# Windowed attention's softmax in the first stage: the exponentials taken by group of 64 keys on ScalarE, in place of a shift and a sum on VectorE

## What is computed

```python
attn = jnp.einsum('bhnd,bhmd->bhnm', q, k)
bias = bias_table[REL_IDX.reshape(-1)].reshape(N, N, NH).transpose(2, 0, 1)
attn = jax.nn.softmax(attn + bias[None], axis=-1)
out = jnp.einsum('bhnm,bhmd->bhnd', attn, v)
```

## Time and profile before

| | us |
|---|---|
| median of three runs | 798.73 |
| lowest and highest | 797.12, 801.46 |
| the profiled execution | 798.17 |
| its span (first to last instruction) | 796.4 |
| granted clock of TensorE, mean of the span | 0.906 |

### The profile page before, as it was taken

The page is one execution under the profiler, slowest core; times in us unless marked ns, Lnnn a source line. Parts: engine busy times, 40 slices in busy tenths (PEclk is TensorE's granted clock), DMA queues, the critical chain, the costliest instruction groups (busy, mean ns, idle before and its releaser), DMA issues.

```text
span 796.4 us, 20147 instructions
## 1 busy us (share of the span) xinstructions
PE 639.5 (80%) x8800; PEld 538.0 (68%) x8800; DVE 498.0 (63%) x1102; ACT 328.0 (41%) x510; POOL 208.4 (26%) x193
## 2 busy tenths in 40 slices
PE   5355797979797979687479576899999899989776
PEld 5345576868686868665368465678787787868665
DVE  2267678687878787821445353558677776847455
ACT  3134343443435343400697514453536355342420
POOL 0100000000000000000468542635446373633330
PEclk8575899999999999898599798889999999989898
DMA  5120301010101000000112403213140413220000
GB/s 206 54 74 1 119 14 38 15 38 16 37 16 37 2 2 2 2 1 12 55 32 63 66 14 54 51 18 64 18 81 15 68 34 48 49 33 2 14 15 14
DMA packets 28263, 29.76 MB, mean 37 GB/s; under 512 B 1936, under 2 KB 22544, under 8 KB 28048
## 3 DMA queue, kind: packets, MB, share of 16 engines
q1 hardware_dynamic: 28176, 28.49, 15.8%
HBM read 22.19 MB, written 6.29 MB: 36 GB/s over the span
## 4 chain that ended last, share of the span: by engine, by line
PE 31%; DVE 7%; ACT 5%; POOL 3%; DMA 3%; issue 2%; SPq 1%; DVEq 0%; POOLq 0%; ACTq 0%
PE ps L214 17%; PE ps L1050 3%; PE ps L1002 3%; DMA ks<-rope_scratch 2%; PE ps L1028 2%; DVE mx L1318 2%; PE ps L1031 2%; POOL hl L1224 1%; PE ps L1034 1%; PE ps L1005 1%; PE ps L913 1%; ACT wide L1138 1%; DVE acc L1408 1%; SPq L897 1%; DVE st L1260 1%
## 5 line engine op out<-in xcount | busy, mean ns | idle before, releaser
L1238 POOL TENSOR_TENSOR e2l<-prob,e2h 128x1536 f16<-128x1536 f32 x32 | 98.7, 3103 | 18.5 <-ACT e2h L1173 18.5
L214 PE MATMUL ps<-secondh,ch_moe 128*128 128x256 f16 (+1 forms) x320 | 82.6, 266 | 3.3 <-DVE cl_moe L1271 3.0
L214 PE MATMUL ps<-yh,wconvh 128*128 128x256 f16 x288 | 80.7, 280 | 3.3 <-DVE yl L755 3.3
L214 PE MATMUL ps<-secondh,cl_moe 128*128 128x256 f16 (+1 forms) x320 | 82.7, 265 | 0.0
L1318 DVE TENSOR_REDUCE mx<-ps 128x2 f32<-128x512 f32 (+1 forms) x96 | 65.4, 682 | 27.1 <-PE ps L1005 27.1
L214 PE MATMUL ps<-secondl,ch_moe 128*128 128x256 f16 (+1 forms) x320 | 82.4, 264 | 0.0
L214 PE MATMUL ps<-yh,wconvl 128*128 128x256 f16 x288 | 80.9, 281 | 0.0
L214 PE MATMUL ps<-yl,wconvh 128*128 128x256 f16 x288 | 80.5, 280 | 0.0
L635 POOL TENSOR_TENSOR rstd<-mv,eps 128x4 f32<-128x4 f32 x8 | 1.6, 201 | 265.7 <-DVE mv L660 265.7
L1167 ACT ACTIVATE prob<-ps 128x1536 f32<-128x1536 f32 x32 | 46.5, 1452 | 54.3 <-PE ps L1034 54.3
L1408 DVE SCALAR_TENSOR_TENSOR acc<-ps,gate,acc 128x256 f32<-128x256 f32 x112 | 49.0, 479 | 21.7 <-PE ps L214 21.7
(11 more groups left out here) (217 smaller groups left out, 2117.5 us busy)
## 6 DMA issues: line engine op xcount, KB each, us to landing
weights_stage<-in_second SPq DMA_DIRECT2D x6, 684.0 KB, 4.2
qs<-rope_scratch SPq DMA_DIRECT2D x48, 64.0 KB
ks<-rope_scratch SPq DMA_DIRECT2D x48, 64.0 KB
weights_stage<-in_wconv SPq DMA_DIRECT2D x6, 384.0 KB, 3.7
xw<-in_xw SPq DMA_DIRECT2D x8, 256.0 KB, 2.7
xc<-in_xc SPq DMA_DIRECT2D x8, 256.0 KB, 2.6
rope_scratch<-rh SPq DMA_DIRECT2D x8, 256.0 KB, 2.3
rope_scratch<-rl SPq DMA_DIRECT2D x8, 256.0 KB, 2.3
```

The source lines that it names most:

```text
L214: last = nc.tensor.matmul(out_ap, lhs[x], rhs[w], start=done == 0, stop=done == n - 1)
L1238: nc.gpsimd.tensor_tensor(el[n % 2][:], prob[n % 2][:], eh[n % 2][:], ALU.subtract).then_inc(e2_lo, 1)
```

## The change

In `scores`, VectorE no longer subtracts the maxima from the tile: it changes the sign of the 16 maxima of each half (an instruction over 128 x 16 in place). ScalarE then takes the exponential of each group of 64 keys by an instruction of its own, with the negated maximum of that group as the bias (a pointer to a column of 128 numbers), and each of these instructions also writes the sum of its 64 results to a column of `sums`. There are 16 for each half, 32 for each image and 256 in all, where there were 2 and 16. The semaphore `exp_done` is raised by the last of each sixteen. In `turn`, VectorE's sum and the wait on it go.

```diff
+                rows = prob[:].rearrange("p (g m) -> p g m", m=WTOK)
                 for at in range(2):
-                    act.wait_ge(shifted[p], i * 2 + at + 1)
-                    e = prob[:, at * 2 * BANK:(at + 1) * 2 * BANK]
-                    nc.scalar.activation(e, e, ACT.Exp).then_inc(exp_done[p], 1)
+                    act.wait_ge(negated[p], i * 2 + at + 1)
+                    for g in range(at * 16, at * 16 + 16):
+                        last = nc.scalar.activation(rows[:, g], rows[:, g], ACT.Exp, bias=mx[:, g:g + 1],
+                                                    accum_out=sums[:, g:g + 1])
+                    last.then_inc(exp_done[p], 1)
...
                 for at in range(2):
                     dve.wait_ge(max_done[p], i * 2 + at + 1)
-                    nc.vector.tensor_tensor(rows[:, at], rows[:, at],
-                                            mx[:, at * 16:(at + 1) * 16].unsqueeze(2).to_broadcast([P, 16, WTOK]),
-                                            ALU.subtract).then_inc(shifted[p], 1)
+                    columns = mx[:, at * 16:(at + 1) * 16]
+                    nc.vector.tensor_scalar(columns, columns, -1.0, None, ALU.mult).then_inc(negated[p], 1)
...
-                rows = prob[:].rearrange("p (g m) -> p g m", m=WTOK)
                 dve.wait_ge(exp_done[p], i * 2 + 2)
-                nc.vector.tensor_reduce(sums[:], rows, op=ALU.add, axis=AX).then_inc(sum_done[p], 1)
-                dve.wait_ge(sum_done[p], i + 1)
                 nc.vector.reciprocal(rs[:], sums[:]).then_inc(recip_done[p], 1)
```

More of the change, by code:

```diff
@@ L360, in windows @@
         (x_loaded, dct_done, stats_done, mv_done, eps_added, rstd_done, norm_done, tr_done, affine_done, xh_done,
-         xl_done, qk_done, qkh_done, qkl_done, v_done, vh_done, vl_done, scores_done, biased, max_done, shifted,
+         xl_done, qk_done, qkh_done, qkl_done, v_done, vh_done, vl_done, scores_done, biased, max_done, negated,
          exp_done, et_done, eh_done, el_done, pv_done, recip_done, o_done, oc_done, och_done, ocl_done, y_done,
@@ L365, in windows @@
                               "tr_done", "affine_done", "xh_done", "xl_done", "qk_done", "qkh_done", "qkl_done",
-                              "v_done", "vh_done", "vl_done", "scores_done", "biased", "max_done", "shifted",
+                              "v_done", "vh_done", "vl_done", "scores_done", "biased", "max_done", "negated",
                               "exp_done", "et_done", "eh_done", "el_done", "pv_done", "recip_done", "o_done",
@@ L369, in windows @@
                               "conv_done", "z_done"))
-        sum_done = sems("sum_done")
         pads_set, half_set = sem("pads_set"), sem("half_set")
```

## The result

The changed kernel took 864.13 us (median of four runs, 862.52 to 865.41) against 800.1 us for the kernel before on the same chip: a ratio of 1.080, 95% interval 1.076 to 1.085, so 8% slower. The forecast was 885 us with a range of 838 to 926. The profiled execution took 862.52 us, and its span is 860.7 us, 64.3 us longer than the span before.

A forecast was written before the change was run, and what follows sets the result against it. TensorE sets the pace, and the end of ScalarE's exponentials fixes when its convolution starts. Terms of 67.7 + 6.8 + 12.0 = 86.5 us on the profiled 798.2 us gave 885 us, range 838 to 926.

The forecast's parts named there:

- What bounds the kernel: In the inner turns, the end of ScalarE's exponentials, through `yh`, fixes the convolution's start; each microsecond it moves lengthens the turn.
- Part 1: On VectorE, two shifts of 1.215 us become two negations of about 175 ns; exponentials start 1.03 us earlier.
- Part 2: On ScalarE, 32 exponentials at 0.40 us take 12.8 us: `yh` 9.67 us later in seven turns, image 0 6.8 us.
- the sum of 86.5: Total predicted loss in us: 67.7 for seven turns, 6.8 for image 0, 12.0 for TensorE's clock.
- Part 3: VectorE's sum, 2.27 us an image, goes; worth nothing, since TensorE's work covers it in the inner turns.
- Part 4: TensorE's clock falls to half rate behind longer idles: 2.0 us in each of images 1 to 6, 12.0 us.
- the free sum: On ScalarE, writing the sum costs nothing: step 0.24 us, 842 us in all; chance 0.18.
- the serial one: On ScalarE, the sum is a full instruction without overlap: step 0.56 us, 926 us in all; chance 0.17.
- The faster one: ScalarE's queue hides small instructions' fixed part: step nears 0.05 us, 786 us in all; chance 0.03.
- TensorE's wait: Sign in the profile after: TensorE's wait at L494 for ScalarE's exponentials rises from 24.0 to some 100 us.

The follow-up runs named there:

- finer order: Next image's statistics ahead of the maxima, exponentials (half of them in the changed kernel) behind `to_channels`, values before weighing: kernel before 781.85 us, changed kernel 811.60 us.
- pairs of groups: Changed kernel with maxima, exponentials and sums over 128 elements, 16 for an image, not computing the reference's softmax: 823.71 us, ratio 1.030.
- first order of the experiments: `y`, `yh`, `yl` ahead of maxima and exponentials, both convolutions ahead of the transposes: kernel before 830.17 us, changed kernel 820.55 us.

## Why the prediction was right, and where its sizes were off

*What bounds the kernel.* Right: the end of the exponentials, through `yh`, sets the turn. Where `yh` starts later, the turn lengthens by that and the clock, from 37.6 to 47.1 us (161.21 to 208.27); the six turns from image 1's `yh` to image 7's lengthen by 8.6 to 9.8 us, where I had 10 to 12. In the finer order, where `yh` stands ahead, the changed kernel's shortest turn is 37.4.

*Part 1.* Right. Two negations span 0.29 us (169 ns each by the profile), and the exponentials of image 3 start 0.19 us behind the start of the first negation (197.46 to 197.65); I had 0.22.

*Part 2.* Right in kind, off in size. The step without a sum, 0.24 us by the rows of before, was 0.24 in the run without sums. The sum is a second instruction, for which I had no row. I took the middle of 0.24 and 0.56 us, 0.40; it is 0.331. The read overlaps on both sides (it starts 0.24 us behind the start of an exponential of 0.33 us, and the next one starts 0.09 us behind it) and so adds 0.09 us; my own figure for that case was 0.35. This is the term that was mis-sized: 0.069 x 32 is 2.2 us a turn, so that seven times 9.67 us were seven times 7.47, and image 0 cost 4.9 in place of 6.8. That is 17 of the 22 us by which the sum of 86.5 was above the 64.3 measured; 2 more are the clock, and the rest is what was given back ahead of the first softmax and in the last part.

*What the Trainium skill said of it.* The Trainium skill, in "VectorE: DVE Perf Modes", section "Two Vector instructions with no wait between them", says of Vector instructions that one which writes its accumulator out is two, the main one and a read. By this case's trace it is so on ScalarE too: 256 rows of ACTIVATION_READ_ACCUMULATOR, 187 ns each. The Trainium skill's rule in the same page's section on the TRN2 errata, that an SBUF source's fixed latency is exposed between instructions, would by my estimate have made the step 0.345 without the sum. The measured 0.24 says that part of it is hidden, as the rows of before had it. The same section of the Trainium skill says that many small tiles pay that latency each time. The pairs of groups agree: half the count gave back 40 us.

*Part 3.* Right: with the sum gone and 32 us off VectorE (I had some 34), nothing can be seen to have come of it in this order; the runs that gave VectorE its sum or its shift back were both faster. What I had not seen is that this is a property of the order: in the first order of the experiments the shift stood ahead of `xn` and the sum ahead of `el`, and their removal paid.

*Part 4.* Right: 10.3 us by the pieces (11.3 in images 1 to 6, for which I had 12.0, less 1.0 in image 7, for which I had nothing), and by the run with idle matmuls 10.4 us (8.4 by the ratios, 1.080 and 1.070). The granted clock was 0.50 behind the waits.

*Of the rivals* the free sum (842 us) and the serial one (926 us) are excluded by the step. The serial one's case was that the read waits for its exponential, but it starts before the exponential's recorded end. The faster one needed a step under 0.10 us; it was 0.24 even without the sum.

*TensorE's wait* for the exponentials rose to 74.9 us, not to some 100. I had two idles a turn, 7.5 and 5.4 us; in image 3 they were 6.60 and 3.27. The shorter step took about 1 us off each, and the first eight transposes, which I had at 1 us at full rate, took 1.94 at half rate and so filled 0.9 us more of the second.

## What to carry to other kernels

Price work that is moved to an idle engine by the queue that it enters: look for the instruction behind it that a busy engine needs next, and count instructions, not elements. A busy share of 41% said that ScalarE had room, and the one place where it had none was this. Before such a trade, try the order. Here the same swap cost 64 us in one order. In another it gave 10, but only because that order had made the kernel before 35 us slower. The best order without the swap was worth 14 us, and no order tried with the swap reached the kernel before.

## What the runs showed of the hardware

On ScalarE a sum of results costs an instruction of 187 ns that adds 0.09 us to the step of exponentials over 128 x 64; a bias pointer adds about as much (249 against 333 ns for 128 x 64); and an exponential over 128 x 64 starts each 0.24 us with one of the two and each 0.33 us with both. A half-rate stretch of TensorE could be bought off with idle matmuls in the waits, 8 to 10 us for 392 of them.
